# Graph attention on one core: the order of work within a step, on TensorE, VectorE and ScalarE

## What is computed

```python
q = (h @ Wq + bq).reshape(n, 16, 8) * 16 ** -0.5
k = (h @ Wk + bk).reshape(n, 16, 8)
v = (h @ Wv + bv).reshape(n, 16, 8)
s = jnp.einsum('edh,edh->eh', q[row], k[col])          # a score for each edge and head
m = jax.ops.segment_max(s, row, num_segments=n)
p = jnp.exp(s - m[row])
z = jax.ops.segment_sum(p, row, num_segments=n)
attn = p / z[row]
out = jax.ops.segment_sum(attn[:, None, :] * v[col], row, num_segments=n)
x = _layernorm(x + out)
```

## Time and profile before

| | before |
|---|---|
| median of three runs | 2050.88 us |
| span of the profiled execution, first to last instruction | 2508.7 us |
| busy in the span: PE, DVE, ACT, POOL | 1711.0, 1503.7, 1071.4, 1420.0 us |
| instructions of PE, DVE, ACT, POOL | 10160, 4756, 2202, 1482 |
| gathers on POOL: layer 0, layer 1 (twice 312), attention | 416, 624, 416 |
| first gather of attention, last gather, end | 1757.9, 2437.0, 2508.7 us |

### The profile page before, as it was taken

One profiled execution on the slowest core, in us unless ns is written; L12 is line 12 of the kernel. 1 busy time (PEld: TensorE's weight loads), 2 busy tenths in 40 slices (PEclk: granted clock), 3 DMA queues, 4 the chain that ended last, 5 costly groups with the idle time before them and its releaser, 6 DMA issues.

```text
span 2508.7 us, 36098 instructions
## 1 busy us (share of the span) xinstructions
PE 1711.0 (68%) x10160; PEld 1376.1 (55%) x10160; DVE 1503.7 (60%) x4756; ACT 1071.4 (43%) x2202; POOL 1420.0 (57%) x1482
## 2 busy tenths in 40 slices
PE   3668777777387888785688888986236565565567
PEld 2556656666366766664566666754124454454456
DVE  6556555555467776676366666677445565565666
ACT  2234435545556655665244444433332232332332
POOL 6666666665466665563566666612755555555540
PEclk9555555556688998897789999998555555555555
DMA  5121221212123342332323333222544344344340
GB/s 154 46 75 49 74 74 48 73 49 70 45 80 85 87 113 55 108 90 70 116 68 107 111 87 113 84 96 64 163 130 126 116 132 125 113 135 122 115 120 6
DMA packets 171435, 231.75 MB, mean 92 GB/s; under 512 B 48220, under 2 KB 123983, under 8 KB 170980
## 3 DMA queue, kind: packets, MB, share of 16 engines
q0 software_dynamic: 53376, 123.02, 18.0%
q1 hardware_dynamic: 116710, 104.76, 14.1%
q10 hardware_dynamic: 1154, 1.67, 0.2%
HBM read 196.52 MB, written 36.08 MB: 93 GB/s over the span
## 4 chain that ended last, share of the span: by engine, by line
PE 38%; another core or an unknown queue 20%; DVE 15%; issue 15%; ACT 8%; SPq 2%; DVEq 1%; DMA 1%; ACTq 0%
PE p_g L801 9%; PE p_d L924 6%; PE p_d L813 5%; PE p_g L911 5%; PE p_d L853 4%; PE p_o L834 2%; ACT oht L2124 2%; DVE S L1385 1%; PE p_g L894 1%; DVE hs L2258 1%; PE p_g L887 1%; DVE Sb L1420 1%; DVE work L1503 1%; DVE work L1489 1%
## 5 line engine op out<-in xcount | busy, mean ns | idle before, releaser
L734 POOL DMA_INDIRECT G<-h_d,idx x624 | 608.8, 976 | 414.7 <-issue 158.4
L2003 POOL DMA_INDIRECT G<-kv_d,idx x416 | 395.7, 951 | 323.1 <-DVE PV L2311 169.2
L734 POOL DMA_INDIRECT G<-in_x,idx x416 | 401.1, 964 | 215.6 <-issue 107.5
L801 PEld LDWEIGHTS p_g<-S,G 128*128 128x128 f32 x2080 | 377.6, 245 | 212.8 <-issue 174.7
L801 PE MATMUL p_g<-S,G 128*128 128x96 f32 (+1 forms) x2080 | 397.0, 325 | 138.8 <-issue 134.7
L1412 DVE TENSOR_TENSOR agg<-agg,p_g 128x96 f32 (+1 forms) x520 | 119.8, 230 | 331.9 <-remote 208.8
L924 PE MATMUL p_d<-Sb,kv_s 128*128 128x288 f32 x728 | 244.8, 458 | 85.3 <-ACT kv_s L1156 46.6
L1503 DVE TENSOR_TENSOR work<-work,p_d 128x312 f32 (+1 forms) x416 | 180.8, 465 | 155.0 <-remote 68.9
L1385 DVE SCALAR_TENSOR_TENSOR S<-con,rel,shared 128x96 f32<-128x96 f32 (+1 forms) x1040 | 261.8, 293 | 0.4
L813 PE MATMUL p_d<-work 128*128 128x312 bf16 (+1 forms) x832 | 201.1, 371 | 61.7 <-issue 30.8
L1164 ACT ACTIVATE work<-con,lo_f 128x128 bf16<-128x128 f32 x416 | 143.0, 392 | 227.8 <-PE p_d L813 119.7
(11 more groups left out here) (324 smaller groups left out, 3246.2 us busy)
## 6 DMA issues: line engine op xcount, KB each, us to landing
dst_b<-in_dst_row SPq DMA_DIRECT2D x104, 240.0 KB
work<-A_d SPq DMA_DIRECT2D x25, 800.0 KB
A_d<-work SPq DMA_DIRECT2D x12, 1600.0 KB
G<-h_d,idx POOLq DMA_INDIRECT x624
G<-in_x,idx POOLq DMA_INDIRECT x416
kv_s<-low_d SPq DMA_DIRECT2D x52, 128.0 KB
G<-kv_d,idx POOLq DMA_INDIRECT x416
kv_s<-low_d SPq DMA_DIRECT2D x52, 96.0 KB
```

Source lines behind the costliest of these rows:

```text
L734: pool.indirect_dma_start(G[:, n % GRING, :], None, l.table, bass.IndirectOffsetOnAxis(ap=l.places[:, c:c + 1], axis=0)).then_inc(s_arr[i ...
L801: last = pe.matmul(p_g[:, g % PB, 0:width], G[:, c % GRING, :], S[:, c % (SRING * GR), 0:width], start=(k == 0), stop=(k == GR - 1))
L2003: pool.indirect_dma_start(G[:, c % KRING, :], None, d["kv"], bass.IndirectOffsetOnAxis(ap=idx[:, c:c + 1], axis=0)).then_inc(s_arr[c // QC ...
```

## The change

In a step, TensorE issues `rows` right behind `scores_t`, `columns` behind the first group's `queries`, `weights_back` and `difference` behind the second group's; of the four node sums the first stays ahead of `scores_t`, and the other three come behind `difference`. ScalarE's `weights_copy` and `fade` come right behind `weights`, ahead of `deviation` and of the last two groups' one-hots. VectorE's `chunk_max`, `row_max` and `segment_max` come earlier against `head_part`, `products` and `outputs`, and its `add`s of the old batch later; `values(4k-3)` stays last. What is computed is the same, and so are the instructions. Orders on GpSimd and SyncE are unchanged.

```diff
--- before.py
+++ after.py
@@ -2084,26 +2084,24 @@
                     window_sums(4 * k - 8)
                 if mid:
                     scores_t(k - 1)
+                    rows(k - 1)
                 if now:
                     queries(4 * k)
-                if old:
-                    window_sums(4 * k - 7)
+                if mid:
+                    columns(k - 1)
                 if now:
                     queries(4 * k + 1)
-                if mid:
-                    rows(k - 1)
-                if old:
-                    window_sums(4 * k - 6)
-                if now:
-                    queries(4 * k + 2)
-                if mid:
-                    columns(k - 1)
-                if old:
-                    window_sums(4 * k - 5)
                 if mid:
                     weights_back(k - 1)
                     if k > 1:
                         difference(k - 1)
+                if old:
+                    window_sums(4 * k - 7)
+                if now:
+                    queries(4 * k + 2)
+                if old:
+                    window_sums(4 * k - 6)
+                    window_sums(4 * k - 5)
                 if now:
                     queries(4 * k + 3)
                 for t in in_step(k):
@@ -2187,23 +2185,20 @@
                     rows_copy(k - 1)
                     rows_ordered(k - 1)
                     columns_copy(k - 1)
-                for t in in_step(k - 1):
-                    deviation(t)
                 if nxt:
                     far(4 * k + 5)
                     hot(4 * k + 5)
                 if mid:
                     weights(k - 1)
-                if nxt:
-                    far(4 * k + 6)
-                    hot(4 * k + 6)
-                if mid:
                     weights_copy(k - 1)
                     if k > 1:
                         fade(k - 1)
-                if nxt:
-                    far(4 * k + 7)
-                    hot(4 * k + 7)
+                for t in in_step(k - 1):
+                    deviation(t)
+                for q in (4 * k + 6, 4 * k + 7):
+                    if nxt:
+                        far(q)
+                        hot(q)
         passes(act, ns, turn, body)
 
     def vector(dve, turn_sums):
@@ -2379,40 +2374,44 @@
                     values(4 * k - 6)
                     if k > 2:
                         rescale(k - 2)
+                if mid:
+                    chunk_max(k - 1)
+                if old:
                     add(4 * k - 8)
                 if now:
                     products(4 * k, landed)
                 if mid:
-                    chunk_max(k - 1)
+                    row_max(k - 1)
+                if old:
+                    values(4 * k - 5)
+                if batch(k + 2):
+                    one_hots(k + 2)
+                if mid:
+                    segment_max(k - 1)
                 if now:
                     head_part(4 * k)
+                if mid and k > 1:
+                    fade_log(k - 1)
+                if now:
+                    products(4 * k + 1, landed)
                 for t in in_step(k - 1):
                     outputs(t)
-                if mid:
-                    row_max(k - 1)
-                if batch(k + 2):
-                    one_hots(k + 2)
+                if now:
+                    head_part(4 * k + 1)
                 if old:
                     add(4 * k - 7)
-                    values(4 * k - 5)
                 if now:
-                    products(4 * k + 1, landed)
-                    head_part(4 * k + 1)
+                    products(4 * k + 2, landed)
+                    head_part(4 * k + 2)
                 if mid:
-                    segment_max(k - 1)
+                    values(4 * k - 4)
                 if old:
                     add(4 * k - 6)
                 for t in in_step(k - 1):
                     normalise(t)
-                if now:
-                    products(4 * k + 2, landed)
-                    head_part(4 * k + 2)
                 if old:
                     add(4 * k - 5)
                 if mid:
-                    if k > 1:
-                        fade_log(k - 1)
-                    values(4 * k - 4)
                     values(4 * k - 3)
             dve.reg_add(turn, turn, 1)
             dve.wait_ge(s_end, dve.snap(turn, min_val=1, max_val=1000) * 4)
```

## The result

| | before | after |
|---|---|---|
| median | 2052.86 us (5 runs, 2049.81 to 2054.32) | 2061.38 us (5 runs, 2056.72 to 2064.30) |
| ratio | | 1.0040, 95% interval 1.0025 to 1.0055 |
| span of the profiled execution | 2508.7 us | 2059.6 us |

The changed kernel is slower by 8.5 us, 0.4%. The forecast was 2092 us, 41 more, with a range of 2050 to 2126: the direction was right, the size five times too large.

The account below looks back on a forecast made before the run. GpSimd's unpaused gathers were taken to bound the kernel, everything else hiding behind them. 36 us for steps longer than the gathers' limit plus 5.5 us at the end made +41.5 on 2050.9: 2092 us, range 2050 to 2126.

Parts of the forecast that it names:

- the holds: Waits of ScalarE's L2134 after TensorE's L2030 had ended, 10.1 us of a 26.7 us step, taken as absent from timed runs.
- the chain: Dependent work across TensorE, ScalarE and VectorE, from transposing scores to the transpose back, in each new step: 7.5 us.
- the loop: The changed kernel's whole step without gathers: 7.5 us of linked work plus 12.7 us of other TensorE work, 20.2 us.
- the drain: Work behind the last transpose of scores: 35.5 us before, 41 us forecast after, +5.5 us.
- rival (1): TensorE's clock rises to 2.4 GHz in its dense piece, the gathers bind again: 2048 us, 6 in 100.
- Rival (4): Timed runs have the hold too, and it ends 3 us sooner in the new order: 1985 us, 8 in 100.
- the limit of 18.7 us a step: Longest attention step that still hides behind the gathers, 448.5 us over 24 steps; each microsecond above it costs 24.
- the 36 us of the sum: Loss forecast in attention's steps: 20.2 - 18.7 = 1.5 us a step, 24 times.
- The signs of being wrong: Last steps shorter than 18.7 us, a rising clock, or timed gathers quicker than 1.25 us.
- Rival (2): Links overlap more than counted, the step stays under 18.7 us, only the end moves: 2051 to 2060 us, 18 in 100.
- the hold taken from 26.7 us: The kernel before's attention step in the held trace, 26.7 us less 10.1 us of waiting, given as some 16.3 us.
- 1820 + 190.3 + 37.7: 1456 gathers at 1.25 us, gaps between their streaks, and work after the last: 2048.0 us against 2050.9 timed.

Follow-up runs that it names:

- e1: The kernel before, unchanged, run again for a new trace (also written e1_before): 2049.96 us, ratio 0.9994 to the kernel before.
- e4: The kernel before with two of four gathers of each group left out from the 17th group on (also e4_half_before): 1968.44 us, ratio 0.9599.
- e7: The changed kernel with two more scans into a spare tile ahead of the first two in `chunk_max`: 2075.91 us, ratio 1.0119 to before.
- e3_drain_new: The kernel before's order while batches are new, the changed kernel's order only behind them, on three engines: 2058.28 us, ratio 1.0031 to before.
- e6_one_back: The changed kernel with one node sum put back into TensorE's chain ahead of `columns`: 2054.40 us, ratio 1.0018 to before.
- e5: The changed kernel with two of four gathers of each group left out from the 17th group on: 2060.30 us, ratio 1.0037 to before.

## Why the prediction was wrong

**Right:** that timed runs are paced by the gathers and the holds belong to one profiled execution (e1, e4); the chain, 7.5 us forecast and 7.48 measured; the loop, 20.2 forecast and 20.0 measured; TensorE idle before L2034 and L2049; the drain, +5.5 forecast and +5.9 measured; the clock, 0.50 from attention's first scores on, so that rival (1) falls; the 24 us for each microsecond above the limit, which e7 shows. The chain is right part by part too (1.92 us from the transpose to ScalarE's copy, 2.62 to `columns`, 2.94 to `weights_back`; forecast 1.95, 2.51, 3.05), so its sum is no luck. Rival (4), faster by a shorter hold, falls with the hold.

**The step that failed is the limit of 18.7 us a step,** and with it the 36 us of the sum. It is 20.0 in e1_before, and 19.8 to 19.9 behind a late start (e3_drain_new, after). It was worked out as 448.5 us for 24 steps; e1_before has 479.4. Three terms of it were mis-sized:

| | prediction | e1_before | difference |
|---|---|---|---|
| gathers of attention, first to last | 520 | 532.6 | +12.6 |
| last gather to the last scores | 5.1 | 4.1 | -1.0 |
| first gather to the second batch's scores, taken off | 76.6 | 57.3 | +19.3 |
| for 24 steps | 448.5 | 479.4 | +30.9 |

The third is the largest. I took the start of attention from the held trace, took off 2 us of it for a hold, and kept the rest; but that execution was stretched there too, by 16.2 us up to the first scores (1811.5 - 1757.9 = 53.6, against 1511.83 - 1474.45 = 37.4), and the next batch came 19.9 us behind and not 23. No other trace comes near 76.6: the latest start, in e6_one_back, has 64.3. The first is small in each piece: most gathers do take 1.25 us, but 17 of 416 follow the one before after more than 1.5, and the mean is 1.28. I had the range of the loop (14.7 to 21.6) with care and the limit with none, although the time hung on the difference of the two, 1.5 us out of 20, times 24. An error of 1.3 us on the limit, 24 times, makes 31 of the 36 us, and the 0.2 by which the loop was taken too long the other 5; the late start of the changed kernel's executions gives back the 3.1 measured in the steps. The signs of being wrong named quicker gathers, which would lower the limit, and none that would raise it. Rival (2) came near the time, 2051 to 2060 at 18 in 100, but for another reason: it had the loop shorter, not the limit longer. The measured 2061.38 lies just above it, 2059.32 in it.

That 2061.38 lies in the range of 2050 to 2126 as well is owed to that rival's place in it, not to the sum. Two smaller slips of the prediction: the hold taken from 26.7 us leaves 16.6, not 16.3, though e4_half_before has 16.4; and the forecast's lower end, 2063 for a step of 19.2, leaves out the drain's 5.5.

**Why the check by the total did not warn.** 1820 + 190.3 + 37.7 came within 2.9 us of the timed run, and I took that as proof of every term. The terms had errors of opposite sign. In e1_before the streaks of gathers last 530.0 + 409.9 + 401.7 + 532.6 = 1874.2 us, 54 more than 1820, and the gaps between them (15.7, 18.4 and 93.6, with 5.3 ahead) 133.0 us, 57 less than 190.3: the held execution had stretched the gaps as well. The third term, 37.7 behind the last gather, is 39.5 (2007.10 to 2046.6). The pace that I derived from the sum was right as a mechanism and wrong by 0.03 us a gather.

**The profile's scale.** I expected the span after to be 2530 to 2610, with the holds. It was 2059.6. Nor are the holds in attention all of the excess: the first gather of attention starts at 1757.9 in the held trace and at 1474.45 in e1_before, so 283 of the 462 us between the two spans arose ahead of it. What makes such an execution was not found out; the unchanged kernel gave a trace without holds, so they do not come with the old order each time.

## What to carry to other kernels

When one engine paces a stretch and the others follow, a reordering is to be judged by two numbers, the new loop's own length and the pace-maker's, and the time depends on their difference: both need the same care; here 1.3 us in 20 decided it. A sum that matches the total within 2.9 us of 2051 supports the mechanism at most; it does not prove its terms, and above all not where they are read in a profile that is longer than the timed run. Here the order lost all its slack, 3.6 us a step, for a price of 3 us in the steps, and the next 0.65 us of work a step cost 16: slack that costs nothing today is worth keeping. If a profile's span is far from the time, take another before anything else.

## What was not expected of the hardware

- Two profiled executions of one kernel had spans of 2508.7 and 2046.6 us. In the longer one 21 of attention's 26 hand-overs from TensorE's L2030 to the ScalarE copy that waits for it took 9.3 to 10.6 us, and one 2.65; in the other 25 of 26 took 0.04 us. The first is of another kind in both (14.8 and 3.2 us): ScalarE is then behind with its one-hots.
- The profiled execution of e6_one_back had a span of 3178.4 us, in a kernel whose other executions took some 2054. Its excess lies ahead of attention: attention's first gather starts at 2597.39 instead of 1474.45, and its 416 gathers then take 530.9 us, as ever. TensorE's 728 products of L924, all ahead of attention, took 0.92 us each in it and 0.42 in after. Its page reports a mean granted clock of 1.000 but has no row of the clock by slice, so that figure is not to be relied on. What made it was not found out.
- From attention's first scores on TensorE stayed at the lower clock (0.50) in every trace with a row of the clock, in after with 354.9 us of matmuls in 479.8 and a dense piece of 12 us in every step. The rule of the Trainium skill, "TensorE: Matmul & The Clock Gate", section "Why this matters for your kernels", that continuous work brings the full clock, is not borne out for this mix by any of these traces.
- Gathers of 128 rows of 1 KB followed each other on GpSimd at 1.25 us (median start to start) in every trace of attention, with half of them left out too (1.251 in e4, 1.257 in e5, where GpSimd also waits for places in the ring). Some come later: the means over the four streaks of gathers of e1_before are 1.275 to 1.315 us.
